# First layer of a two-layer kernel: another table of half-steps, with four stores and loads moved in SyncE's program and the products of steps 2 and 10 on GpSimd in place of 1 and 14

## The chip, the cores and the metric

The kernel runs on one core of one Trainium2 chip. The metric is the device time of one execution in microseconds, lower is better. Engines are named as in the profile: PE is TensorE's matmul (PEld its weight load), DVE is VectorE, ACT is ScalarE, POOL is GpSimd, SP (SPq in the rows) is SyncE, whose program does nothing but issue DMAs here.

## The reference, cut to what matters

Layer 0 is a windowed selective scan. The 4x128x128x128 input is cut into 8x8 windows of 64 tokens. Layer 1 is a spectral operator with a two-layer perceptron behind it; the change doesn't touch it.

```
tn = layernorm(t); xi, z = split(tn @ W_in + b_in)
xc = silu(causal_conv4(xi) + conv_b)
dr, Bm, Cm = split(xc @ W_x);  delta = softplus(dr @ dt_w + dt_b)
for each token:                                   # h: 256 channels x 16 states
    h = exp(delta * A) * h + (delta * xc) * Bm
    y = sum over the 16 states of h * Cm
y = (y + xc * D) * silu(z);  out = y @ W_out + b_out;  x1 = out + x
# layer 1: layernorm over channels, rfft2, filters, irfft2, mixing by Theta, MLP, + x1
```

## The kernel before, in words

Layer 0 works on 64 blocks, each one row of 16 windows (1024 tokens, 128 channels on the partitions). A block is 32 steps: step `n` is state `n % 16` of one half (`q = n // 16`) of the block's tokens. In a step the scan (DVE, L922) runs over 128x1024 elements with `decay` (exp(delta*A), ACT, L737) and `drive` (delta*xc*B) as inputs and writes `state`. `prod` is `state` times C, and TensorE transposes and adds each `prod` into `y_acc` (L612, `add_state`, three steps behind the scan).

Two tables say who makes what. In the even steps (`DSTEPS`) the decay lies in one PSUM buffer `decay_d`, and GpSimd makes `drive_d` (L1081) from `du` and a row of B that a DMA has broadcast into one of four `b_all`. In the odd steps ACT scales `ut` into `ub` (L750, four instructions) and PE turns it into the one buffer `drive_r` (L599, `turn_drive`). For steps in `BY_GPSIMD` the product is GpSimd's (L1092) with a row of C that a DMA has broadcast into one of four `c_all`; for the nine others it is DVE's (L933), with C broadcast by PE into `job_bank0` (L587, `broadcast_c`).

Around the scans each engine does the block's other work at half-steps: `h = 2n` is before the product at step `n`, `h = 2n + 1` behind it. `JOBS` gives PE's jobs, as (half-step, name, kind, bank): two PSUM banks are shared, a job waits until the job before it in its bank was taken, and a job in bank 0 also waits for every product of DVE of the steps before. A name's last two digits are the channel half and `q`. `mean`/`var` belong to the layernorm of the block two ahead (L629, L635), `conv`, `z`, `xp` (L641, L645, L652), `dt` (L658, the argument of softplus), `ut` and `bt` (L670, L664) prepare a block's second half or the next block, `turn` (L675 and L679) brings y back to channels, `out` (L689, L691) projects it, `fy` (L696) belongs to layer 1. `AT` gives the half-step at which ACT, DVE or GpSimd takes a job's result, and the step at which SP issues a store or an x load. All engines run their programs in order, so a wait holds everything behind it. SP's program is one queue too: `load_b` runs 8 steps ahead of its drive and `load_c` 6 steps ahead of its product, each behind a wait for its buffer, and the stores (`rows`, x1, `yo`) stand between them:

```
if n == AT["yo_out"] and S.tail:
    need(sp, s["yo_done"], m - 1)      # counted by ACT at half-step 63 of this block
    sp.dma_start(yv[...], yo[:])
...
if kind of a job: if S.bank[name] == 0:
    need(pe, s["prod_v_done"], m * len(BY_VECTOR) + nth(BY_VECTOR, n))
```

Of the kernel before, what the change touches and what calls it, by code (L numbers as in the profile page):

```python
# [62 lines left out]
RSTEPS = tuple(n for n in range(NSTEP) if n not in DSTEPS)  # L63
ALLSTEPS = tuple(range(NSTEP))
UB_AT = {}
BY_GPSIMD = (1, 3, 4, 5, 7, 8, 9, 11, 12, 13, 14, 15, 17, 18, 19, 21, 23, 24, 25, 26, 27, 29, 31)
BY_VECTOR = tuple(n for n in ALLSTEPS if n not in BY_GPSIMD)
NB, NCR, NA, ND, NS_UB, NT, NP = 4, 4, 2, 4, 2, 4, 4
B_LOAD, C_LOAD, ADD_BEHIND = 8, 6, 3
# [2 lines left out]

JOBS = [
# [8 lines left out]
]  # L82
CONV_GAP = 2
UT_BY_SCALAR = ('ut10', 'ut01', 'ut00')
Z1_BY_VECTOR = ()

AT = {

    "copy_y": (37, 8), "take_rows": (37, 2), "take_conv": (9, 19, 28, 31), "take_z": (4, 1, 18, 21),
    "softplus0": 39, "softplus1": 12, "silu": 33, "take_bt": (59, 21), "square": (43, 51), "deviation": (46, 55),  # L90
# [1 line left out]

# [2 lines left out]

# [1 line left out]

    "x_in": 17, "rows": (21, 0), "rows_landed": (22, 2), "x1_out": 15, "x_res": 14, "yo_out": 28,
}


# [5 lines left out]
def upto(steps, M, n):  # L107

    return M * len(steps) + nth(steps, n + 1)
# [7 lines left out]
def place_of(steps, M, n, ring):  # L117
    return (M * len(steps) + nth(steps, n)) % ring


def before_in(steps, M, n, ring):

    i = M * len(steps) + nth(steps, n) - ring
    return i // len(steps), steps[i % len(steps)]
# [46 lines left out]
def need(eng, sem, value):  # L171

    if isinstance(value, int) and value <= 0:
        return
    eng.wait_ge(sem, value)  # L175
# [232 lines left out]
def layer0(nc, a, wt, rows_dram, x1_dram, y_dram, blocks):  # L408
    with ExitStack() as ctx:
# [86 lines left out]
        def multiplied(eng, M, n):  # L496
            if n in BY_VECTOR:
                need(eng, s["prod_v_done"], upto(BY_VECTOR, M, n))
            else:
                need(eng, s["prod_g_done"], upto(BY_GPSIMD, M, n))  # L500

# [6 lines left out]
        def _(sp):  # L508
# [10 lines left out]
            def load_b(step):  # L519
                M, p, n = step  # L520
                q, st, slot = n // NS, n % NS, place_of(DSTEPS, M, n, NB)
                need(sp, s["drive_d_done"], upto(DSTEPS, *before_in(DSTEPS, M, n, NB)))
                sp.dma_start(b_all[slot][:], rows_dram[2 * p + q, st:st + 1, :].to_broadcast([P, HT])).then_inc(b_ready[slot], 16)

            def load_c(step):
                M, p, n = step
                q, st, slot = n // NS, n % NS, place_of(BY_GPSIMD, M, n, NCR)
                need(sp, s["prod_g_done"], upto(BY_GPSIMD, *before_in(BY_GPSIMD, M, n, NCR)))
                sp.dma_start(c_all[slot][:],
                             rows_dram[2 * p + q, NS + st:NS + st + 1, :].to_broadcast([P, HT])).then_inc(c_ready[slot], 16)  # L530
# [6 lines left out]
            def body(S, p):  # L537
# [3 lines left out]
                for n in range(NSTEP):  # L541
# [26 lines left out]
                    for k in range(NSTEP):  # L568
                        if k in DSTEPS and (k - B_LOAD) % NSTEP == n and S.step(n + B_LOAD, p):
                            load_b(S.step(n + B_LOAD, p))  # L570
                        if k in BY_GPSIMD and (k - C_LOAD) % NSTEP == n and S.step(n + C_LOAD, p):
                            load_c(S.step(n + C_LOAD, p))
# [153 lines left out]
        def _(act):  # L726
# [39 lines left out]
            def take_ut(S, hf, q):  # L766
                misc = full(act, S, f"ut{hf}{q}")
                act.activation(ut[q][:, :, hf * P:(hf + 1) * P], misc[:].rearrange("p (g d) -> p g d", g=4),
                               ACT.Copy).then_inc(take(S, f"ut{hf}{q}"), 1)
# [74 lines left out]
            def others(S, p, h):  # L844
# [9 lines left out]
                for hf in range(2):  # L854
                    if h == AT["take_ut1"][hf] and S.scan and f"ut{hf}1" in UT_BY_SCALAR:
                        take_ut(S, hf, 1)
                    if h == AT["take_ut0"][hf] and S.front and f"ut{hf}0" in UT_BY_SCALAR:
                        take_ut(S, hf, 0)
# [51 lines left out]
        def _(dve):  # L910
# [63 lines left out]
            def take_ut(S, hf, q):  # L974
                misc = full(dve, S, f"ut{hf}{q}")
                dve.tensor_copy(ut[q][:, :, hf * P:(hf + 1) * P],
                                misc[:].rearrange("p (g d) -> p g d", g=4)).then_inc(take(S, f"ut{hf}{q}"), 1)

            def take_dt(S, hf, q):
                M = S.m + 1 if q == 0 else S.m  # L980
                misc = full(dve, S, f"dt{hf}{q}")
                need(dve, s["softplus_done"], M * 8 + 4 * q + 4)
                need(dve, s["decay_d_done"], upto(DSTEPS, M - 1, NS * (q + 1) - 1))
                need(dve, s["decay_r_done"], upto(RSTEPS, M - 1, NS * (q + 1) - 1))
                need(dve, s["du_done"], (M * 2 + q - 1) * 2)
                dve.scalar_tensor_tensor(delta[:, hf, q * HT:(q + 1) * HT], misc[:], 0.0, soft[:, hf, :], ALU.max,
                                         ALU.add).then_inc(take(S, f"dt{hf}{q}"), 1)
# [31 lines left out]
            def others(S, p, h):  # L1019
# [5 lines left out]
                for hf in range(2):  # L1025
                    if h == AT["take_dt1"][hf] and S.scan:
                        take_dt(S, hf, 1)
                    if h == AT["take_dt0"][hf] and S.front:
                        take_dt(S, hf, 0)
                    if h == AT["take_ut1"][hf] and S.scan and f"ut{hf}1" not in UT_BY_SCALAR:  # L1030
                        take_ut(S, hf, 1)
                    if h == AT["take_ut0"][hf] and S.front and f"ut{hf}0" not in UT_BY_SCALAR:
                        take_ut(S, hf, 0)
# [39 lines left out]
        def _(pool):  # L1073
# [11 lines left out]
            def times_c(step):  # L1085
                M, p, n = step
                slot = place_of(BY_GPSIMD, M, n, NCR)
                M0, n0 = before_in(ALLSTEPS, M, n, NP)
# [563 lines left out]
```

## Time and profile before

| | |
|---|---|
| median of 3 runs | 9224.3 us (9222.76 to 9227.81) |
| the profiled execution | 9230.91 us, its span 9229.1 us |
| busy over the span | PE 92%, DVE 88%, ACT 83%, POOL 87% |
| layer 0 | about the first 6,650 us of the span |

The profile is one execution. A block of layer 0 is some 45 instructions on POOL, 73 on DVE, 180 on ACT. Rows name a buffer without its number, and a matmul of 512 columns of this type is counted twice (x2). PEclk is TensorE's granted clock: 1.00 is its level of 2.4 GHz and 0.50 that of 1.2 GHz.

### The profile page before, as it was taken

The page shows a single profiled execution, that of the slowest core. Times are in us where ns is not written, and L with a number is a line of the kernel's source. Part 1 is how long each engine was busy: PE and PEld are TensorE (multiplying, and loading weights), DVE is VectorE, ACT ScalarE, POOL GpSimd, SP SyncE. Part 2 cuts the span into 40 slices and gives each one's busy share as a digit, 9 for nine tenths or more (in the row PEclk, how much of TensorE's full clock was granted, in tenths as well). Part 3 has the DMA queues.
Part 4 walks back from the last instruction along what each step waited for, and adds up shares of the span by engine and source line. Part 5 has one row for each costly group of instructions (what it writes and reads, how often), then busy time and mean ns, then how long its engine had stood idle before and what let it go on. Part 6 is the DMA issues. An engine that isn't in the chain of part 4 may idle for free. (4 is left out here: it accounts for less than half of the span.)

```text
span 9229.1 us, 157478 instructions
## 1 busy us (share of the span) xinstructions
PE 8530.3 (92%) x52285; PEld 6506.9 (71%) x52285; DVE 8123.3 (88%) x8018; ACT 7644.1 (83%) x13862; POOL 8028.2 (87%) x3673
## 2 busy tenths in 40 slices
PE   6998999999999999999999999999799999999999
PEld 3666666666666666666666666666589999999788
DVE  5989988999999899989998999899789999999766
ACT  5999999999999999999999999999755555555577
POOL 4999999999999999999999999999889999999500
PEclk8999999999999999999999999999999999999999
DMA  3333334343434343434343433343310110110255
GB/s 92 118 123 127 121 121 128 120 123 120 128 120 125 120 127 118 124 120 127 120 124 119 127 120 124 120 126 122 113 36 33 37 37 33 37 37 33 89 185 182
DMA packets 675841, 982.03 MB, mean 106 GB/s; under 512 B 82762, under 2 KB 280403, under 8 KB 670931
## 3 DMA queue, kind: packets, MB, share of 16 engines
q1 hardware_dynamic: 675282, 974.98, 33.6%
q8 instruction: 302, 4.95, 0.2%
q14 instruction: 257, 2.10, 0.1%
HBM read 828.71 MB, written 146.04 MB: 106 GB/s over the span
## 5 line engine op out<-in xcount | busy, mean ns | idle before, releaser
L1092 POOL TENSOR_TENSOR prod<-state,c_all 128x1024 f32<-128x1024 f32 x1472 | 3476.0, 2374 | 95.5 <-DMA b_all<-bc_rows 54.4
L922 DVE TENSOR_TENSOR_SCAN state<-decay_r,drive_r 128x1024 f32<-128x1024 f32 x1024 | 2331.0, 2276 | 302.3 <-ACT decay_r L737 199.3
L1081 POOL TENSOR_TENSOR drive_d<-du,b_all 128x1024 f32<-128x1024 f32 x1024 | 2422.5, 2366 | 173.8 <-issue 142.7
L922 DVE TENSOR_TENSOR_SCAN state<-decay_d,drive_d 128x1024 f32<-128x1024 f32 x1024 | 2332.1, 2277 | 38.9 <-ACT decay_d L737 36.5
L612 PEld LDWEIGHTS y_acc<-ident,prod 128*128 128x128 f32 x16384 | 1918.5, 144 | 601.4 <-issue 531.1
L612 PE MATMUL y_acc<-ident,prod 128*128 128x128 f32 x16384 | 2207.0, 280 | 17.6 <-POOL prod L1092 11.5
L1369 DVE SCALAR_TENSOR_TENSOR sum_d<-bank_d,filt,sum_d 128x512 f32<-128x512 f32 x2470 | 1654.2, 742 | 119.8 <-PE bank_d L1277 119.8
L750 ACT ACTIVATE ub<-ut,bt 128x256 f32<-128x256 f32 x4096 | 1737.5, 497 | 9.3
L1416 POOL TENSOR_TENSOR sum_p<-sum_p,scaled 128x1024 f32<-128x1024 f32 x650 | 1555.2, 2393 | 79.9 <-ACT scaled L1327 32.2
L1327 ACT ACTIVATE scaled<-bank_p,filt 128x512 f32<-128x512 f32 x1560 | 944.5, 689 | 622.5 <-PE bank_p L1277 592.7
L737 ACT ACTIVATE decay_r<-delta,neg_a 128x504 f32<-128x504 f32 x2048 | 1342.0, 704 | 0.0
L737 ACT ACTIVATE decay_d<-delta,neg_a 128x504 f32<-128x504 f32 x2048 | 1310.1, 672 | 22.9 <-DVE state L922 21.1
L599 PE MATMUL drive_r<-ident,ub 128*128 128x128 f32 x8192 | 1076.0, 275 | 33.2 <-DVE state L922 27.8
L599 PEld LDWEIGHTS drive_r<-ident,ub 128*128 128x128 f32 x8192 | 928.9, 141 | 228.3 <-issue 175.2
L641 PE MATMUL job_bank<-tn,tap_w 128*128 128x512 f32 (+3 forms) x2048 | 965.9, 594 | 2.3 <-ACT zs L779 1.6
L1277 PE MATMUL bank_d<-th_high,x_high 128*128 128x256 f32 x2600 | 781.0, 300 | 6.2 <-DVE sum_d L1369 1.9
L933 DVE TENSOR_TENSOR prod<-state,job_bank 128x1024 f32<-128x1024 f32 x576 | 694.9, 1206 | 95.4 <-issue 52.5
L1277 PE MATMUL bank_d<-th_low,x_high 128*128 128x256 f32 x2600 | 735.5, 283 | 0.0
L1277 PE MATMUL bank_d<-th_high,x_low 128*128 128x256 f32 x2600 | 735.4, 283 | 0.0
L641 PEld LDWEIGHTS job_bank<-tn,tap_w 128*128 128x128 f32 x2048 | 350.2, 191 | 291.0 <-issue 272.7
L1277 PEld LDWEIGHTS bank_d<-th_high,x_high 128*128 128x128 f32 x2600 | 492.7, 190 | 37.3 <-DVE sum_d L1369 20.3
L1277 PEld LDWEIGHTS bank_d<-th_low,x_high 128*128 128x128 f32 x2600 | 492.3, 189 | 16.9 <-issue 15.3
(156 smaller groups left out, 13507.0 us busy)
## 6 DMA issues: line engine op xcount, KB each, us to landing
c_all<-bc_rows SPq DMA_DIRECT2D x1472, 256.0 KB, 3.3
b_all<-bc_rows SPq DMA_DIRECT2D x1024, 256.0 KB, 3.7
ys<-row_spectra SPq DMA_DIRECT2D x130, 256.0 KB, 2.8
column_sums<-tt SPq DMA_DIRECT2D x130, 256.0 KB, 2.2
x_in<-in_x_dram SPq DMA_DIRECT2D x64, 512.0 KB, 5.6
x_res<-in_x_dram SPq DMA_DIRECT2D x64, 512.0 KB, 4.3
x_rows<-x SPq DMA_DIRECT2D x64, 512.0 KB, 3.5
row_spectra<-z SPq DMA_DIRECT2D x64, 512.0 KB, 3.7
```

Source lines behind the costliest of these rows:

```text
L599: mm = pe.matmul(drive_r[:, hf, g * P:(g + 1) * P], ub[place_of(RSTEPS, M, n, NS_UB)][:, g, hf * P:(hf + 1) * P], wt["ident"][:], start=Tr ...
L612: mm = pe.matmul(y_acc[:, g, hf * P:(hf + 1) * P], prod[place_of(ALLSTEPS, M, n, NP)][:, hf, g * P:(g + 1) * P], wt["ident"][:], start=(n ...
L641: mm = pe.matmul(o[:, :, k:WT], wt["tap_w"][:, K - 1 - k, hf * P:(hf + 1) * P], v[:, :, 0:WT - k], start=(k == 0), stop=(k == K - 1), skip ...
L737: last = act.activation(dst[:, hf, :, 1:WT], delta[:, hf, q * HT:(q + 1) * HT].rearrange("p (w t) -> p w t", t=WT)[:, :, 1:WT], ACT.Exp, s ...
L750: last = act.activation(ub[place_of(RSTEPS, M, n, NS_UB)][:, g, :], ut[q][:, g, :], ACT.Copy, scale=bt[q][:, g, st:st + 1])
L922: dve.tensor_tensor_scan(state[place_of(ALLSTEPS, M, n, NT)][:].rearrange("p h t -> p (h t)"), decay[:].rearrange("p h w t -> p (h w t)"), ...
L1081: pool.tensor_tensor(drive_d[place_of(DSTEPS, M, n, ND)][:], du[:, :, q * HT:(q + 1) * HT], b_all[slot][:].unsqueeze(1).to_broadcast([P, 2 ...
L1092: pool.tensor_tensor(prod[place_of(ALLSTEPS, M, n, NP)][:], state[place_of(ALLSTEPS, M, n, NT)][:], c_all[slot][:].unsqueeze(1).to_broadca ...
L1277: mm = pe.matmul(o, x[p][:, part, b, :], th[:, 2 * pair:2 * pair + 2, :].rearrange("p l h -> p (l h)"), start=(b % 2 == 0 and i == 0), sto ...
L1327: act.activation(scaled[n % 2][:, i, out, :].rearrange("p (b h) -> p b h", b=B), bank_p[:, :, i, :], ACT.Copy, scale=filt[p][:, kind, 2 * ...
L1369: dve.scalar_tensor_tensor(acc, src, factor, acc, ALU.mult, ALU.add).then_inc(s["summed_d"], 1)
L1416: pool.tensor_tensor(acc, acc, scaled[n % 2][:, i], ALU.add).then_inc(s["summed_p"], 1)
```

## The change

`BY_GPSIMD` loses steps 1 and 14 and gains 2 and 10, so DVE's nine products are those of steps 0, 1, 6, 14, 16, 20, 22, 28, 30 (before: 0, 2, 6, 10, 16, 20, 22, 28, 30). `ut01` is taken by DVE instead of ACT. `JOBS` and `AT` get other half-steps nearly throughout; no work is added or removed. The core of the diff:

```diff
-BY_GPSIMD = (1, 3, 4, 5, 7, 8, 9, 11, 12, 13, 14, 15, 17, 18, 19, 21, 23, 24, 25, 26, 27, 29, 31)
+BY_GPSIMD = (2, 3, 4, 5, 7, 8, 9, 10, 11, 12, 13, 15, 17, 18, 19, 21, 23, 24, 25, 26, 27, 29, 31)
...
-    (15, "conv10", "front", 1), (16, "z01", "front", 0), (18, "ut01", "scan", 0), (20, "bt1", "scan", 0),
-    (20, "z11", "front", 1), (22, "conv01", "front", 1), (23, "ut11", "scan", 0), (25, "conv11", "front", 0),
-    (29, "out0", "back", 1), (31, "out1", "back", 0), (34, "xp0", "front", 1), (37, "dt10", "front", 0),
-    (38, "dt00", "front", 1), (40, "mean0", "ahead", 1), (45, "var0", "ahead", 0), (48, "ut00", "front", 0),
+    (15, "bt1", "scan", 1), (16, "z11", "front", 0), (16, "conv10", "front", 1), (20, "z01", "front", 0),
+    (22, "ut01", "scan", 1), (23, "ut11", "scan", 0), (24, "conv01", "front", 1), (25, "conv11", "front", 0),
+    (30, "out0", "back", 1), (31, "out1", "back", 0), (34, "xp0", "front", 1), (37, "dt00", "front", 1),
+    (38, "dt10", "front", 0), (41, "mean0", "ahead", 1), (44, "var0", "ahead", 0), (47, "ut00", "front", 0),
...
-UT_BY_SCALAR = ('ut10', 'ut01', 'ut00')
+UT_BY_SCALAR = ('ut10', 'ut00')
...
-    "x_in": 17, "rows": (21, 0), "rows_landed": (22, 2), "x1_out": 15, "x_res": 14, "yo_out": 28,
+    "x_in": 16, "rows": (18, 0), "rows_landed": (24, 2), "x1_out": 21, "x_res": 19, "yo_out": 31,
```

Three places of the new order matter below. On PE, around the `mean0` job (L629) in the second half of a block; L658 are the two `dt` jobs, L635 is `var0`, L670 is `ut00`, L612 the adds, L599 the turned drives, L587 the broadcasts of C. Before:

```order
L658 MATMUL job_bank<-rows,dt_w 128x512 x2
L612 MATMUL y_acc<-ident,prod 128x128 x8
L599 MATMUL drive_r<-ident,ub 128x128 x8
L629 MATMUL job_bank<-x_in,centre_w 128x512
L612 MATMUL y_acc<-ident,prod 128x128 x8
L587 MATMUL job_bank<-c_rows,pick 128x512
L612 MATMUL y_acc<-ident,prod 128x128 x8
L599 MATMUL drive_r<-ident,ub 128x128 x8
L612 MATMUL y_acc<-ident,prod 128x128 x8
L635 MATMUL job_bank<-sq,mean_w 128x512
L587 MATMUL job_bank<-c_rows,pick 128x512
```

And now:

```order
L658 MATMUL job_bank<-rows,dt_w 128x512 x2
L612 MATMUL y_acc<-ident,prod 128x128 x8
L599 MATMUL drive_r<-ident,ub 128x128 x8
L612 MATMUL y_acc<-ident,prod 128x128 x8
L629 MATMUL job_bank<-x_in,centre_w 128x512
L587 MATMUL job_bank<-c_rows,pick 128x512
L612 MATMUL y_acc<-ident,prod 128x128 x8
L599 MATMUL drive_r<-ident,ub 128x128 x8
L635 MATMUL job_bank<-sq,mean_w 128x512
L612 MATMUL y_acc<-ident,prod 128x128 x8
L587 MATMUL job_bank<-c_rows,pick 128x512
L612 MATMUL y_acc<-ident,prod 128x128 x8
L670 MATMUL job_bank<-ident,du 128x128 x4
```

One add moved ahead of `mean0`, and `var0` moved ahead of an add. `ut00` (L670) now follows the broadcast for step 22 with one add between.

On SP, at the end of a block, around the store of `yo` (L554); L523 loads a row of B, L529 one of C, L534 and L535 store a half block's rows. Before:

```order
L523 DMA b_all<-bc_rows 128x512
L529 DMA c_all<-bc_rows 128x512
L554 DMA row_spectra<-z 128x8x128
L523 DMA b_all<-bc_rows 128x512
L529 DMA c_all<-bc_rows 128x512 x2
L523 DMA b_all<-bc_rows 128x512
L529 DMA c_all<-bc_rows 128x512
L534 DMA bc_rows<-rows 16x512
L535 DMA bc_rows<-rows 16x512
```

And now:

```order
L523 DMA b_all<-bc_rows 128x512
L529 DMA c_all<-bc_rows 128x512 x2
L523 DMA b_all<-bc_rows 128x512
L554 DMA row_spectra<-z 128x8x128
L529 DMA c_all<-bc_rows 128x512
L534 DMA bc_rows<-rows 16x512
L535 DMA bc_rows<-rows 16x512
```

The store stands behind the loads of B for steps 4 and 6 and of C for 2, 3 and 4 now, where it stood ahead of B for 4 and 6 and of C for 3, 4 and 5.

On DVE, in the middle of a block, steps 10 to 16 (scans L922, `decay_d` in even steps; L933 a product; L976 a take of `ut`). Before:

```order
L922 SCALAR_TENSOR_TENSOR state<-decay_d,drive_d 128x1024
L922 SCALAR_TENSOR_TENSOR state<-decay_r,drive_r 128x1024
L933 TENSOR_TENSOR prod<-state,job_bank 128x1024
L922 SCALAR_TENSOR_TENSOR state<-decay_d,drive_d 128x1024
L976 COPY ut<-job_bank 128x4x128
L922 SCALAR_TENSOR_TENSOR state<-decay_r,drive_r 128x1024
L922 SCALAR_TENSOR_TENSOR state<-decay_d,drive_d 128x1024
L922 SCALAR_TENSOR_TENSOR state<-decay_r,drive_r 128x1024
L1004 TENSOR_TENSOR x<-job_bank,out_b_rows 128x512
```

And now:

```order
L922 SCALAR_TENSOR_TENSOR state<-decay_d,drive_d 128x1024
L922 SCALAR_TENSOR_TENSOR state<-decay_r,drive_r 128x1024
L976 COPY ut<-job_bank 128x4x128 x2
L922 SCALAR_TENSOR_TENSOR state<-decay_d,drive_d 128x1024
L922 SCALAR_TENSOR_TENSOR state<-decay_r,drive_r 128x1024
L922 SCALAR_TENSOR_TENSOR state<-decay_d,drive_d 128x1024
L922 SCALAR_TENSOR_TENSOR state<-decay_r,drive_r 128x1024
L933 TENSOR_TENSOR prod<-state,job_bank 128x1024
```

Both takes of `ut` now stand between scans 11 and 12, and a product follows scan 15 instead of scan 11.

## Rows read from the trace of the kernel before

**Rows 1.** Layer 0: stretch, its length, busy PE, PEld, DVE, ACT, POOL, PEclk, DMA.

```profile
1000.00:3000.00 2000.00, 1830.46 (x10742) 1295.98 (x10743) 1819.42 (x1406) 1874.90 (x3494) 1885.64 (x881) 0.98 0.39 123
```

**Rows 2.** The same view for three whole blocks.

```profile
3893.79:3995.07 101.28, 92.74 (x552) 66.12 (x549) 92.87 (x73) 95.73 (x179) 96.70 (x46) 0.98 0.40 124
4097.86:4201.20 103.34, 94.61 (x552) 66.48 (x550) 92.84 (x73) 95.81 (x179) 96.33 (x46) 0.97 0.40 121
2776.00:2876.20 100.20, 91.48 (x551) 64.89 (x550) 92.56 (x73) 95.72 (x180) 96.29 (x45) 1.00 0.41 125
```

**Rows 3.** Who waited for whom, 2000 to 4000 us: total us, times, longest.

```profile
DVE state L922 <- ACT decay_r L737: 63.3, 20, 3.2
POOL drive_d L1081 <- issue: 49.1, 16, 3.9
PE job_bank L675 <- DVE delta L986: 40.7, 19, 2.1
```

**Rows 4.** The same view for SP's own queue.

```profile
SPq L554 <- ACTq L842: 163.1, 20, 8.5
```

**Rows 5.** SP in order of time, turn of a block: start us, us, instruction.

```profile
3894.52 0.39 SPq L554 DMA_DIRECT2D row_spectra<-z  x1
3894.95 0.58 SPq L523 DMA_DIRECT2D b_all<-bc_rows  x1
```

**Rows 6.** POOL in order of time; [idle before <-releaser].

```profile
3900.62 2.36 POOL L1081 TENSOR_TENSOR drive_d<-du,b_all 128x1024 f32<-128x1024 f32 x1 [2.76 <-issue]
```

**Rows 7.** Busy time in three stretches of the block that starts at 3893.87.

```profile
3893.87:3916.72 22.85, 20.62 (x111) 13.28 (x109) 22.09 (x15) 22.36 (x43) 20.09 (x10) 1.00 0.51 138
3916.72:3954.90 38.18, 38.07 (x237) 28.27 (x237) 31.70 (x27) 36.79 (x67) 38.18 (x20) 1.00 0.34 114
3967.13:3995.14 28.01, 25.26 (x169) 19.08 (x167) 27.78 (x19) 24.44 (x50) 27.32 (x13) 0.99 0.27 87
```

**Rows 8.** PE in order of time, the wait for `dt01` in this block.

```profile
3916.72 1.12 PE L675 MATMUL job_bank<-xc,diag_d 128*128 128x512 f32 x2 [2.15 <-DVE delta L986]
3922.15 1.02 PE L645 MATMUL job_bank<-tn,z_w 128*128 128x512 f32 x2
```

**Rows 9.** The same place one block earlier.

```profile
3813.53 1.70 PE L675 MATMUL job_bank<-xc,diag_d 128*128 128x512 f32 x2 [2.14 <-DVE delta L986]
3820.53 1.02 PE L645 MATMUL job_bank<-tn,z_w 128*128 128x512 f32 x2
```

**Rows 10.** Busy time and granted clock in two short stretches.

```profile
3814.00:3817.40 3.40, 3.40 (x10) 1.83 (x9) 1.26 (x3) 3.40 (x8) 3.40 (x2) 0.51 0.47 159
3964.30:3967.50 3.20, 3.20 (x14) 2.43 (x13) 2.67 (x3) 3.20 (x8) 3.20 (x2) 0.50 0.01 3
```

**Rows 11.** PE in order of time, around `mean0`.

```profile
3958.99 1.09 PE L599 MATMUL drive_r<-ident,ub 128*128 128x128 f32 x8 [0.32 <-DVE state L922]
3962.73 1.12 PE L629 MATMUL job_bank<-x_in,centre_w 128*128 128x512 f32 x2 [2.65 <-DVE delta L986]
3963.69 1.48 PE L612 MATMUL y_acc<-ident,prod 128*128 128x128 f32 x8
3965.10 0.79 PE L587 MATMUL job_bank<-c_rows,pick 48*128 48x512 f32 x1
```

**Rows 12.** DVE in order of time, same place.

```profile
3961.98 1.29 DVE L986 SCALAR_TENSOR_TENSOR delta<-job_bank,soft 128x512 f32<-128x512 f32 x2 [0.34 <-issue]
3963.19 2.28 DVE L922 TENSOR_TENSOR_SCAN state<-decay_r,drive_r 128x1024 f32<-128x1024 f32 x1
3965.99 1.22 DVE L933 TENSOR_TENSOR prod<-state,job_bank 128x1024 f32<-128x1024 f32 x1 [0.53 <-DVE state L922]
```

**Rows 13.** ACT in order of time, same place.

```profile
3960.84 1.06 ACT L791 ACTIVATE soft<-soft 128x1024 f32<-128x1024 f32 x1
3970.38 0.60 ACT L806 ACTIVATE sq<-job_bank 128x512 f32<-128x512 f32 x1 [2.04 <-PE job_bank L635]
```

**Rows 14.** A group of instructions, 2000 to 4000 us: busy us, mean ns, idle before.

```profile
L976 DVE COPY ut<-job_bank 128x512 f32<-128x512 f32 x19 | 12.7, 666 | 0.0
```

More of the change, by code:

```diff
@@ L74 @@
     (0, "z10", "front", 0), (0, "xp1", "scan", 1), (3, "z00", "front", 1), (4, "conv00", "front", 1),
[7 rows of a table removed]
[7 rows of a table added]
 ]
 CONV_GAP = 2
-UT_BY_SCALAR = ('ut10', 'ut01', 'ut00')
+UT_BY_SCALAR = ('ut10', 'ut00')
 Z1_BY_VECTOR = ()
 AT = {
-    "copy_y": (37, 8), "take_rows": (37, 2), "take_conv": (9, 19, 28, 31), "take_z": (4, 1, 18, 21),
-    "softplus0": 39, "softplus1": 12, "silu": 33, "take_bt": (59, 21), "square": (43, 51), "deviation": (46, 55),
[4 rows of a table removed]
-    "x_in": 17, "rows": (21, 0), "rows_landed": (22, 2), "x1_out": 15, "x_res": 14, "yo_out": 28,
+    "copy_y": (37, 7), "take_rows": (35, 2), "take_conv": (10, 20, 30, 32), "take_z": (3, 1, 21, 18),
+    "softplus0": 39, "softplus1": 11, "silu": 34, "take_bt": (57, 15), "square": (44, 53), "deviation": (45, 56),
[4 rows of a table added]
+    "x_in": 16, "rows": (18, 0), "rows_landed": (24, 2), "x1_out": 21, "x_res": 19, "yo_out": 31,
 }
```

14 rows, old and new, of tables (AT, JOBS) are left out of this document.

## The prediction

> **What bounds the kernel now.** I looked first at where the time per block goes. POOL runs 45 instructions a block, so its 881 in 2,000 us are 19.6 blocks, 102.15 us each [rows 1]. POOL is busy 94% of that, ACT 94%, PE and DVE 91%: no engine is full, and the shares don't say which waits set the end. Blocks also differ: 100.20 us where the granted clock is 1.00 all along, 101.28 at 0.98, 103.34 at 0.97 [rows 2]. So I took one block apart and asked of each engine where it has no gap. After its first 22.85 us, in which DVE is busy for 22.09, PE takes over and works 38.07 of 38.18 us without a gap [rows 7]. Then ACT makes the softplus of the next block's first half (its Ln ends at 3961.90 [rows 13]) and DVE's take of it starts at 3961.98 [rows 12]; from the scan at 3967.13 to the next block's first scan DVE is busy for 27.78 of 28.01 us [rows 7]. That is the ring that sets a block: DVE, PE, ACT's softplus, DVE. POOL isn't in it. Its one large gap, 2.76 us ahead of a drive [rows 6] and 2.5 us a block on average (49.1 us in 19.6 blocks [rows 3]), is made by SP: the store of `yo` waits 8.2 us a block for ACT's last instruction of the block (163.1 us, 20 times [rows 4]), and the row of B for step 4 is issued right behind it, at 3894.95 [rows 5], 5.7 us before the drive starts. But the scans don't wait for that drive: no row of scans behind POOL stands among the long waits.
>
> PE itself waits twice in each block for a take by DVE of a `dt` job in its bank: 2.1 us at L675 [rows 3, 8] and 2.65 us at L629 [rows 11]. Behind each the clock can fall. In one block the granted clock was 0.51 after the wait at L675 [rows 10], and from L675 to L645 it took 7.00 us [rows 9]; in the next block, undisturbed, 5.43 [rows 8]: a fall costs 1.57. After the wait at L629 it was 0.50 [rows 10], and the add behind `mean0` took 1.48 us and the broadcast 0.79 [rows 11]. As the 101.28 block has this second fall and no first one, the second costs 101.28 - 100.20 = 1.08 us, and a first one 1.57 to 2.06 (103.34 - 101.28) more [rows 2]. The average of 102.15 is then a second fall in nearly every block and a first one in (102.15 - 101.28) / 2.0, some 45% of them.
>
> **The change part by part.** The products: DVE keeps nine and POOL 23, at 1.2 and 2.3 us each, so no engine's sum changes but by `ut01`, 0.67 us more on DVE and about as much less on ACT [rows 14].
>
> First stretch (DVE, 22.85 us). Product 2 becomes product 1 and `turn10` goes ahead of `turn_drive(5)`. Scan 5 now waits about 1 us for that turn, but the gate that stood behind scan 5 is done in that gap. I come out at 22.9, +0.05.
>
> Middle (PE, 38.18 us). PE's jobs are reordered, none is added; broadcast 10 goes and broadcast 14 comes in the same stretch. Of 38.18 us 0.11 were a wait [rows 7] for the take ahead of broadcast 10: it goes. Is there a new wait? `bt1` stands first now, and ACT must take it before the `conv10` behind it in bank 1; ACT waits there for some 1.3 us instead of at `z01`, and PE not at all by my count. `ut11`, `conv11` and broadcast 14 find their banks taken 0.4 to 1.3 us ahead. DVE has both takes of `ut` ahead of scan 12, 0.67 us each, and product 14 behind scan 15. Scan 15 waits 3.2 us for PE's turned drive (63.3 us over 20 [rows 3]), so both takes are hidden by that wait, and product 14 by PE's 5 us of `out0` and `out1`. Cost 0; uncovered, the takes would be 0.67 us. Value -0.05 for the middle.
>
> Softplus. `take_rows` goes ahead of an ub, so ACT has no other work ahead of the softplus; it still starts with the copy of y, which waits for PE's add 15. The sum gives the end of Ln 0.2 us earlier, with what the middle gave.
>
> Behind the take (the largest term). Product 20 waited for its broadcast, which stood behind `mean0` and an add at the low clock: 0.53 us of wait in the row, and 0.6 from start to start [rows 12]. The add now stands ahead of `mean0`, in PE's wait of 2.65 us, which shrinks by its 0.9 to about 1.75. The broadcast comes right behind `mean0`: by DVE's rows the product can start 3.4 us after the take (1.21 and 2.20 from start to start [rows 12]), and `mean0` and the broadcast need some 2.5 of these, at the low clock. So even a fall there costs nothing, and with the shorter wait it may not come. That is worth 1.08 us in blocks that had it, nearly all: 1.05 on average. `var0` ahead of an add takes ACT's wait of 2.04 us [rows 13] away; since DVE is full there it gives slack, not time. What is late next is `ut00`: it must wait for product 22, now just ahead, about 2.1 us. Behind it stand turned drive 25, `turn01` and `mean1`. Scan 25 wants that drive 2.8 us after product 22 (a scan and a take of `tn`), and `ut00` and the drive need 1.5 at full clock and 3.1 at half: 0 to 0.3, I take 0.1.
>
> SP. The store behind the loads takes POOL's gap of 2.5 us away. No stretch of the ring holds POOL, so I take 0; bounds are 0 and the whole 2.5 (a rival, below). The `rows` store three steps earlier stands behind `take_rows`, done 10 us before; the x loads move by two and five steps and land well ahead.
>
> The first fall. The wait at L675 stays 2.1 us, and nothing says in which blocks the fall behind it comes; with another block length it falls on others. Its bounds are none (-0.9 us a block against now) and all (+1.0, the other 55% at 1.8). I take 60 to 65%, above today's 45%: +0.3.
>
> **The sum**: +0.05 - 0.05 - 0.2 - 1.05 + 0.1 + 0.3 = -0.85 us a block. Over 64 blocks -54 us. Against the profiled execution's own 9230.91 that is 9177; its 6.6 us above the median of 9224.3 are kept, so the median should be 9170. What measurement can tell from no change is about 0.2%, 18 us.
>
> **The rivals.** (1) POOL is what binds, and the moved store is the gain. It is the busiest engine, and its gap is real; against it, its releases come early, and among the long waits none is for it. It would give 2.5 us a block, -160 us: 9064. The Trainium skill (Perfetto Trace Analysis, Identifying the Most-Contended Engine) has it so: the engine with the highest occupancy is the one to optimize first. Here that engine is POOL by a hair, and the rows of the ring speak against it. Chance 5%. (2) No change: the fall behind L675 comes in nearly every block once the other is gone, +1.0 instead of +0.3 a block, and what is left is -0.15 a block, 9214. For it: the wait isn't touched and the block length is what chooses. Chance 14%. (3) Slower, by DVE's middle: with two takes and later the product the scans 12 to 14 run late. If the 3.2 us ahead of scan 15 were used up, because ACT's new wait for `bt1` pushes decays 10 to 14 by more than 3.2 - 1.3 = 1.9 us, each further us would be 64 us: from 0.85 us on the gain is gone, and with 1.4 us it is 35 us slower, 9259. For it: decay 10 and 14 are single-buffered and close behind their scans. Against it: PE reaches `bt1` right behind the first adds. Chance 11%. (4) The fall behind L675 becomes rare: -0.65 us a block instead of +0.3, together -1.8, 9109. Chance 8%.
>
> **Numbers.** The forecast keeps 62%, from 9130 to 9206. With (2) and (4) it holds some eight in ten, so the range is 9105 to 9216. Faster by over 0.2% is the forecast, (1), (4) and a bit more: 0.76; within 0.2% 0.13; slower 0.11.
>
> **What the profile would show.** Right: the wait of ACT for L635 (2.0 us) and DVE's wait ahead of product 20 gone; PE's wait at L629 1.7 to 1.8 us; a new wait of about 2 us at L670; POOL's gap at the drive gone with POOL's other gaps longer by the same; blocks with clock 1.00 at 100.0 us, and others 1.6 to 2 us longer. Wrong: full-clock blocks far below 100 (then POOL was in the ring), or at 101 and more with the wait ahead of scan 15 gone (3), or 102 on average at a clock of 0.97 (2).

## The result: 9153.4 us, 0.8% faster, and the profile after

| | before | after |
|---|---|---|
| median of 4 runs each | 9225.7 us (9222.8 to 9227.8) | 9153.4 us (9148.6 to 9160.7) |
| ratio | | 0.9921, 95% interval 0.9909 to 0.9934 |
| the profiled execution | 9230.9, span 9229.1 | 9160.7, span 9158.9 |

The forecast was 9170 in a range of 9105 to 9216. The change takes off 72 us, where the sum said 54.

The same stretch as in [rows 1], and two blocks one behind the other (columns as there):

```profile
1000.00:3000.00 2000.00, 1842.83 (x10854) 1315.95 (x10855) 1842.82 (x1433) 1886.10 (x3511) 1909.17 (x891) 0.98 0.40 124
2649.42:2749.30 99.88, 91.51 (x551) 65.07 (x549) 93.06 (x74) 95.28 (x178) 96.46 (x46) 1.00 0.40 126
2749.30:2850.81 101.51, 93.97 (x551) 67.84 (x549) 93.24 (x75) 95.26 (x178) 96.53 (x46) 0.97 0.39 124
```

POOL's 891 instructions at 45 a block are 19.8 blocks, 101.0 us each (102.15 before). A block at full clock has gone from 100.20 to 99.88; one with both falls, 103.34 in [rows 2], now lasts 101.51.

PE around `mean0` in the second of these blocks, one with a low clock there, against [rows 11]:

```profile
2816.74 1.04 PE L612 MATMUL y_acc<-ident,prod 128*128 128x128 f32 x8
2819.38 1.13 PE L629 MATMUL job_bank<-x_in,centre_w 128*128 128x512 f32 x2 [1.59 <-DVE delta L986]
2820.43 0.50 PE L587 MATMUL job_bank<-c_rows,pick 48*128 48x512 f32 x1
2820.86 1.80 PE L612 MATMUL y_acc<-ident,prod 128*128 128x128 f32 x8
2822.45 1.91 PE L599 MATMUL drive_r<-ident,ub 128*128 128x128 f32 x8
```

DVE in the same place, against [rows 12]:

```profile
2818.63 1.29 DVE L986 SCALAR_TENSOR_TENSOR delta<-job_bank,soft 128x512 f32<-128x512 f32 x2 [0.16 <-issue]
2819.84 2.28 DVE L922 TENSOR_TENSOR_SCAN state<-decay_r,drive_r 128x1024 f32<-128x1024 f32 x1
2822.03 1.20 DVE L933 TENSOR_TENSOR prod<-state,job_bank 128x1024 f32<-128x1024 f32 x1
```

The wait at L629 is 1.59 us instead of 2.65. The clock falls behind it all the same: the add takes 1.80 us and the turned drive 1.91, about 1.04 at full clock. But the broadcast is out by 2820.93, and product 20 has no wait: 2.19 us from scan to product where it was 2.80. That is the step on which the prediction put most.

The long waits, 2000 to 4000 us, against [rows 3], and SP's own against [rows 4]:

```profile
PE job_bank L675 <- DVE delta L986: 43.2, 20, 2.2
PE job_bank L670 <- issue: 33.0, 20, 2.1
PE job_bank L629 <- DVE delta L986: 31.9, 20, 1.6
DVE state L922 <- PE drive_r L599: 41.8, 50, 3.0
DVE state L922 <- ACT decay_r L737: 27.2, 9, 3.0
```

```profile
SPq L554 <- ACTq L842: 6.8, 20, 0.6
```

The wait at L675 is as long as before, and that at L670 is new, 1.65 us on average. The 3 us ahead of scan 15 is still there; it is put down now to PE, now to ACT. SP waits 0.3 us a block for `yo` instead of 8.2, and POOL has no row of waits for a drive any more.

### The profile page after: what moved, and what is told of

It reads as the page before. It is cut to its first block and busy times, and to the rows that moved or that the text cites. A ratio compares the mean times of both kernels' runs of the same rounds, so it can differ in the third digit from the quotient of the medians.

```text
span 9158.9 us, 157541 instructions
## 1 busy us (share of the span) xinstructions
PE 8504.2 (93%) x52285; PEld 6526.3 (71%) x52285; DVE 8151.9 (89%) x8082; ACT 7618.8 (83%) x13798; POOL 8038.0 (88%) x3673
## 5 line engine op out<-in xcount | busy, mean ns | idle before, releaser
L922 DVE TENSOR_TENSOR_SCAN state<-decay_r,drive_r 128x1024 f32<-128x1024 f32 x1024 | 2328.9, 2274 | 244.7 <-PE drive_r L599 149.9
L922 DVE TENSOR_TENSOR_SCAN state<-decay_d,drive_d 128x1024 f32<-128x1024 f32 x1024 | 2329.8, 2275 | 79.6 <-ACT decay_d L737 79.6
L612 PEld LDWEIGHTS y_acc<-ident,prod 128*128 128x128 f32 x16384 | 1894.1, 143 | 609.5 <-issue 514.1
L612 PE MATMUL y_acc<-ident,prod 128*128 128x128 f32 x16384 | 2199.3, 278 | 20.4 <-POOL prod L1092 6.4
L599 PE MATMUL drive_r<-ident,ub 128*128 128x128 f32 x8192 | 1100.4, 279 | 59.5 <-DVE state L922 40.4
L599 PEld LDWEIGHTS drive_r<-ident,ub 128*128 128x128 f32 x8192 | 946.0, 143 | 199.0 <-issue 136.7
L641 PE MATMUL job_bank<-tn,tap_w 128*128 128x512 f32 (+3 forms) x2048 | 941.3, 587 | 0.8 <-ACT zs L779 0.8
L933 DVE TENSOR_TENSOR prod<-state,job_bank 128x1024 f32<-128x1024 f32 x576 | 691.5, 1200 | 7.2 <-issue 1.8
```

Source lines behind the costliest of these rows:

```text
L599: mm = pe.matmul(drive_r[:, hf, g * P:(g + 1) * P], ub[place_of(RSTEPS, M, n, NS_UB)][:, g, hf * P:(hf + 1) * P], wt["ident"][:], start=Tr ...
L612: mm = pe.matmul(y_acc[:, g, hf * P:(hf + 1) * P], prod[place_of(ALLSTEPS, M, n, NP)][:, hf, g * P:(g + 1) * P], wt["ident"][:], start=(n ...
L641: mm = pe.matmul(o[:, :, k:WT], wt["tap_w"][:, K - 1 - k, hf * P:(hf + 1) * P], v[:, :, 0:WT - k], start=(k == 0), stop=(k == K - 1), skip ...
L922: dve.tensor_tensor_scan(state[place_of(ALLSTEPS, M, n, NT)][:].rearrange("p h t -> p (h t)"), decay[:].rearrange("p h w t -> p (h w t)"), ...
```

## Blocks, and where the clock falls

The averages hide what differs from block to block, so I sorted the same 56 blocks of each profile (the sixth to the sixty-first) by the trace's record of the granted clock. A first fall comes 20 to 30 us into the block, behind L675; a second at 66 to 75 us, at `mean0`; a late one at 76 to 84 us, behind the wait at L670. The table holds the experiments too; ratios are to the kernel before, run on the same chip. "Mean block" is taken over all 63 distances from one block's first scan to the next block's; the falls are counted in the 56. "Clean" is the length of a block without a fall.

| kernel | median us | ratio, 95% interval | mean block | clean (how many) | first | second | late |
|---|---|---|---|---|---|---|---|
| before | 9225.7 | | 102.20 | 100.2 (3) | 27 | 53 | 0 |
| after | 9153.4 | 0.9921 (0.9909 to 0.9934) | 101.05 | 99.9 (21) | 33 | 22 | 7 |
| e1 before + SP's positions | 9223.1 | 0.9999 (0.9990 to 1.0008) | 102.06 | 100.2 (5) | 25 | 51 | 0 |
| e2 before + second half | 9235.3 | 1.0007 (0.9998 to 1.0016) | 102.24 | 100.2 (1) | 54 | 0 | 55 |
| e3 before + first half | 9463.5 | 1.0263 (1.0249 to 1.0277) | 105.88 | none | 4 | 56 | 0 |
| e4 after + add 4 early | 9077.6 | 0.9839 (0.9826 to 0.9853) | 99.76 | 99.5 (19) | 0 | 12 | 25 |
| e5 before + mean0 at 41 | 9188.3 | 0.9948 (0.9935 to 0.9962) | 101.45 | 100.2 (15) | 41 | 23 | 0 |
| e6 before + first half and SP | 9200.6 | 0.9963 (0.9949 to 0.9976) | 101.86 | 99.9 (8) | 27 | 48 | 0 |
| e7 after, mean0 at 40 | 9190.4 | 0.9951 (0.9938 to 0.9965) | 101.69 | none | 31 | 44 | 13 |
| e8 after, yo at 28 | 9203.8 | 0.9979 (0.9970 to 0.9988) | 101.83 | 100.9 (1) | 36 | 10 | 35 |
| e9 after + adds 4, 5 early | 9037.8 | 0.9785 (0.9772 to 0.9798) | 99.10 | 99.0 (45) | 0 | 7 | 4 |
| e10 before + adds 4, 5 early | 9236.3 | 1.0015 (1.0006 to 1.0024) | 102.31 | 100.8 (4) | 1 | 52 | 0 |
| e11 e9, bt1 later | 9033.4 | 0.9794 (0.9781 to 0.9807) | 99.11 | 99.0 (37) | 0 | 11 | 8 |
| e12 e10 + SP's positions | 9166.9 | 0.9932 (0.9918 to 0.9946) | 101.20 | none | 0 | 56 | 0 |

The median of before lay between 9225 and 9236 from one set of runs to the next, so differences below are read from ratios. In e3 and in e8 one more fall, at 39 us of a block, is in no column.

In the kernel before, a block with the second fall alone lasts 101.41 on average and one with both 103.21: 1.21 for the second, 1.80 for the first. In the kernel after, a first fall costs 1.58 (101.45 against 99.87), a second 0.05 (101.50 against 101.45), and a late one 1.0 to 1.4.

## The experiments

**The change in three parts.** The tables fall apart into SyncE's positions, the first half of the block (`BY_GPSIMD`, `UT_BY_SCALAR`, jobs below half-step 34 and what takes them), and the second half.

e1, SyncE's positions alone:

```diff
-    "x_in": 17, "rows": (21, 0), "rows_landed": (22, 2), "x1_out": 15, "x_res": 14, "yo_out": 28,
+    "x_in": 16, "rows": (18, 0), "rows_landed": (24, 2), "x1_out": 21, "x_res": 19, "yo_out": 31,
```

> The kernel before with SyncE's six positions of the change alone (the store of yo at step 31 instead of 28, and the rows, x1 and x loads as changed). My theory: POOL's gap at the drive behind that store goes and nothing else does, so the time stays within 18 us of before's 9225.7. Rival, POOL binds: 2.5 us a block less, 9066. A third way: the scans' times move a little and the clock falls in other blocks, up to 30 us either way.

Measured: no difference. SP's wait for `yo` fell as in the changed kernel, and POOL's gap at the drive is gone:

```profile
SPq L554 <- ACTq L842: 14.1, 20, 1.0
```

```profile
POOL xc L1110 <- ACT xc L779: 53.8, 20, 2.8
```

What POOL won it waits away for ACT, at L1110 (53.8 us over 20 blocks, 2.7 each; 9.9 us in all before), and the block is as long as before. POOL isn't what binds there: the rule of the Trainium skill (Perfetto Trace Analysis, Identifying the Most-Contended Engine) that was rival 1 would have looked in the wrong place, though POOL is the busiest of the four engines in every profile of layer 0 here.

e2, the second half alone (`mean0` 41, `dt00` ahead of `dt10`, `var0` 44, `ut00` 47, `turn01` 48, `mean1` 49, `var1` 54, `bt0` and `ut10` 57, and what takes them):

```diff
-    (38, "dt00", "front", 1), (40, "mean0", "ahead", 1), (45, "var0", "ahead", 0), (48, "ut00", "front", 0),
+    (38, "dt10", "front", 0), (41, "mean0", "ahead", 1), (44, "var0", "ahead", 0), (47, "ut00", "front", 0),
...
```

> The kernel before with the change's positions of the block's second half alone (the add ahead of mean0, dt00 ahead of dt10, var0, ut00, turn01, mean1, var1, bt0, ut10 and what takes them). My theory: this part carries the gain, 1.1 to 1.2 us a block, so about 9225.7 - 72 = 9154, and at the least 9175 if the first clock fall comes in more blocks. Rival, the gain comes from the first half or from the store: within 18 us of before.

Measured: no gain. My theory in that form fell; the rival has the number but not the reason, since e5 below gains 0.52% by one number of this half. Three blocks of it (columns as in [rows 1]):

```profile
2257.37:2359.77 102.40, 94.25 (x552) 66.62 (x550) 92.74 (x73) 95.94 (x179) 96.28 (x46) 0.97 0.37 123
2359.77:2462.16 102.39, 94.22 (x551) 66.58 (x550) 92.74 (x73) 95.92 (x179) 96.28 (x46) 0.97 0.40 123
2567.32:2667.54 100.22, 91.51 (x551) 65.00 (x549) 92.56 (x74) 95.68 (x179) 95.37 (x46) 1.00 0.39 125
```

The second fall is gone in all 56 blocks, as it should be. But the first comes in 54 and a late one in 55, at the same 22.9 and 80.9 us of every block, and each block is 102.4 us long: once this length is reached, it repeats. That is rival 2 of the prediction (the first fall in nearly every block), which the whole change escaped.

e3, the first half alone, with SyncE's positions as before:

```diff
-BY_GPSIMD = (1, 3, 4, 5, 7, 8, 9, 11, 12, 13, 14, 15, 17, 18, 19, 21, 23, 24, 25, 26, 27, 29, 31)
+BY_GPSIMD = (2, 3, 4, 5, 7, 8, 9, 10, 11, 12, 13, 15, 17, 18, 19, 21, 23, 24, 25, 26, 27, 29, 31)
...
```

> The kernel before with the change's first half alone (products 1 and 14 on DVE instead of 2 and 10, bt1, z11, z01, the two takes of ut, turn10, conv, x1). My theory: nothing, since PE's stretch in the middle keeps its jobs: within 18 us of before's 9225.7. Rival, the removed wait ahead of broadcast 10 and the other order carry the gain: about 9155.

Measured: 2.6% slower, which neither the theory nor the rival had. The waits, 2000 to 4000 us, one of SP's among them:

```profile
PE job_bank L629 <- DMA x_in<-in_x_dram: 96.0, 19, 5.4
```

```profile
SPq L562 <- DVE stats L1011: 144.4, 19, 7.9
```

DVE's statistics stand two half-steps later in the new first half. The x1 store at step 15 waits for them, 7.6 us a block instead of 4.4 (87.7 us over 20 before), the x load stands behind it, and PE waits 5 us a block for the x load. The first half can't do without SyncE's positions. Which of them it needs was not run one by one; the waits point to the x1 store and the x load behind it.

e6, the first half with SyncE's positions (the changed kernel with the second half as before):

```diff
-    (38, "dt10", "front", 0), (41, "mean0", "ahead", 1), (44, "var0", "ahead", 0), (47, "ut00", "front", 0),
+    (38, "dt00", "front", 1), (40, "mean0", "ahead", 1), (45, "var0", "ahead", 0), (48, "ut00", "front", 0),
...
```

> The changed kernel with the second half of the block as before, that is the kernel before with the first half and SyncE's positions of the change together. My theory: the 236 us by which the first half alone was slower came from SyncE's old positions, where the x1 store waited 7.9 us for DVE's statistics and held the x load; with the new positions they go, and what is left is the gain of a full-clock block, 0.3 us, with the fall behind mean0 still there: 9225 - 20 = 9205, between 9180 and 9240 by the number of first falls. Rival, the first half is slow with the old second half whatever SyncE does: over 9400.

Measured: 0.37% faster, with clean blocks of 99.9. The 236 us are gone with SyncE's positions, and the 0.3 us of a clean block come from the first half: with SyncE's positions alone (e1) a clean block stays at 100.2.

**The one number.** e5, the kernel before with the add ahead of `mean0`:

```diff
-    (38, "dt00", "front", 1), (40, "mean0", "ahead", 1), (45, "var0", "ahead", 0), (48, "ut00", "front", 0),
+    (38, "dt00", "front", 1), (41, "mean0", "ahead", 1), (45, "var0", "ahead", 0), (48, "ut00", "front", 0),
```

> The kernel before with a single number changed: mean0 at half-step 41 instead of 40, so that the add of step 17 stands ahead of it on PE. My theory, after the run with the whole second half: the wait at L629 shrinks from 2.65 to 1.7 us, the clock fall behind it and the wait ahead of product 20 go, and a block without the first fall lasts 100.2 us instead of 101.4. The time then hangs on the first fall alone: 102.0 us a block if it comes in every block as it did there, which would be 9220, and 101.0 a block, 9150, if it comes in half of them. Rival, the single add does nothing and the other moves of the second half took the second fall away: 9225, with the fall at 70 us into the block still there.

Measured: 0.52% faster, inside the theory's 9150 to 9220. PE's wait and the broadcast behind it:

```profile
2418.81 1.12 PE L629 MATMUL job_bank<-x_in,centre_w 128*128 128x512 f32 x2 [1.79 <-DVE delta L986]
2419.87 0.49 PE L587 MATMUL job_bank<-c_rows,pick 48*128 48x512 f32 x1
```

A second fall costs 0.27 here (102.05 with both, 101.78 with the first alone) instead of 1.21, and comes in 23 blocks instead of 53; the theory had it gone. First falls went from 27 to 41, which gave part of it back.

e7, the reverse: the changed kernel with `mean0` at 40.

```diff
-    (38, "dt10", "front", 0), (41, "mean0", "ahead", 1), (44, "var0", "ahead", 0), (47, "ut00", "front", 0),
+    (38, "dt10", "front", 0), (40, "mean0", "ahead", 1), (44, "var0", "ahead", 0), (47, "ut00", "front", 0),
```

> The changed kernel with mean0 back at half-step 40, ahead of the add of step 17. My theory: the wait at L629 is 2.5 us again and the fall behind it comes in nearly every block and costs about 1.1 us: 9153 + 65 = 9218, less what a different number of first falls gives back. Rival, with product 20's broadcast still early and DVE's order as it is, the fall costs nothing: 9153 to 9165.

Measured: 0.30% slower than the changed kernel, some 27 us where the theory had 65 and the rival at most 12. Second falls went from 22 to 44 and cost 0.8 to 1.0 again (100.7 with the second alone against the changed kernel's 99.9). The gain of e5 and that of e6, 0.52 and 0.37%, add up to the 0.79% of the change within the intervals.

**The store of yo.** e8, the changed kernel with one number back:

```diff
-    "x_in": 16, "rows": (18, 0), "rows_landed": (24, 2), "x1_out": 21, "x_res": 19, "yo_out": 31,
+    "x_in": 16, "rows": (18, 0), "rows_landed": (24, 2), "x1_out": 21, "x_res": 19, "yo_out": 28,
```

> The changed kernel with the store of yo alone back at step 28, ahead of the loads of B and C. My theory: SyncE waits some 8 us a block there again and POOL's drive behind the store is 2 to 3 us late, but no scan waits for it: within 15 us of the changed kernel's 9153. Rival: with product 2 now on GpSimd, whose load of C also stands behind the store, the late row reaches the scans of steps 4 to 6 and costs 1 us a block, 9217.

Measured: 0.6% slower than the changed kernel, some 50 us. My theory fell. The size is near the rival's 64, by another way than it named. One block (PE and DVE at the `ut` jobs, POOL at the drives):

```profile
2053.83 4.71 POOL L1081 TENSOR_TENSOR drive_d<-du,b_all 128x1024 f32<-128x1024 f32 x2 [4.26 <-issue]
...
2084.41 0.63 PE L670 MATMUL job_bank<-ident,du 128*128 128x128 f32 x4 [1.80 <-POOL du L1099]
...
2085.08 0.69 DVE L976 COPY ut<-job_bank 128x512 f32<-128x512 f32 x1 [2.54 <-PE job_bank L670]
```

POOL is 4.26 us late at the drive behind the store. Its `du` of the second channel half (the changed table makes it three half-steps later than before, at 21) comes late, PE waits 1.80 us for it ahead of `ut11`, DVE 2.54 us for `ut11`, and in the changed order both takes stand ahead of scan 12. The average of DVE's wait is 1.2 (23.5 us in 19 waits, against 11.1 in 20). It hangs on the first fall. In the 21 of the 56 blocks without one DVE waits 2.0 us for `ut`, and they last 101.8 on average instead of the changed kernel's 100.0; in the 35 with one, PE comes to `ut11` late anyway, DVE waits 0.65, and they last 101.9 instead of 101.7. So most of the loss is that a block without a first fall is no longer a short one. Late falls came in 35 blocks instead of 7; their share is not told apart.

**The wait at L675.** e4 does to it what the change did to L629. The add of step 4 goes ahead of `turn11`; in the changed kernel it stands behind the broadcast of step 6:

```diff
-                    if S.step(n - ADD_BEHIND, p):
-                        add_state(S.step(n - ADD_BEHIND, p))
+                    for k in [k for k in {6: (3, 4), 7: ()}.get(n, (n - ADD_BEHIND,)) if S.step(k, p)]:
+                        add_state(S.step(k, p))
```

> The changed kernel with one more add moved in the same way: the add of step 4, which stands behind the broadcast for step 6, goes ahead of turn11, into PE's wait of 2.15 us at L675 (the product of step 4 is ready before that wait starts). My theory: the wait shrinks to about 1.3 us, the clock fall behind it goes as that behind mean0 went with a wait of 1.6, and PE's full stretch in the middle has 0.9 us less work: 1.6 us in six of ten blocks and 0.9 in all, 1.8 us a block, 9153 - 115 = 9040. Rival, only the fall goes and something else in the middle takes the 0.9: 9153 - 60 = 9093. Rival, the fall does not depend on this wait: 9153 - 58 = 9095 without any change in the number of falls. Rival, no change: 9153.

e9, the changed kernel with the adds of steps 4 and 5 both early:

```diff
-                    if S.step(n - ADD_BEHIND, p):
+                    for k in [k for k in {6: (3, 4, 5), 7: (), 8: ()}.get(n, (n - ADD_BEHIND,)) if S.step(k, p)]:
```

> The changed kernel with the adds of steps 4 and 5 both ahead of turn11 (the run with the add of step 4 alone gave 9077.6). PE's wait at L675 was 1.3 us there and would be about 0.4. My theory: that run's gain was the first fall and little of PE's 0.9 us (its blocks last 99.5 against 99.9), because the scans of the middle wait 3.0 us for something else by now; a second add then gives nothing in the middle, and the time stays within 15 us of 9078. Rival, PE's stretch in the middle still sets the end: another 0.9 us a block, 9020. Rival, product 5 isn't ready, PE waits for POOL, and it gets slower, 9100.

Measured: 9077.6 and 9037.8 us, 1.6 and 2.15% faster than before. e9's whole stretch and one block of it, and PE at `turn11`:

```profile
1000.00:3000.00 2000.00, 1857.22 (x11093) 1315.34 (x11094) 1878.77 (x1474) 1919.86 (x3577) 1949.76 (x910) 1.00 0.41 127
2496.52:2595.50 98.98, 91.89 (x551) 65.09 (x549) 92.93 (x75) 95.07 (x178) 96.47 (x46) 1.00 0.40 127
```

```profile
2516.17 2.87 PE L612 MATMUL y_acc<-ident,prod 128*128 128x128 f32 x24
2519.37 1.12 PE L675 MATMUL job_bank<-xc,diag_d 128*128 128x512 f32 x2 [0.33 <-DVE delta L986]
...
2521.72 0.52 PE L664 MATMUL job_bank<-ident,rows 88*128 88x88 f32 x4 [0.36 <-DVE gated L992]
...
2532.39 0.63 PE L670 MATMUL job_bank<-ident,du 128*128 128x128 f32 x4 [0.21 <-POOL du L1099]
```

With a wait of 1.3 us (e4) or 0.33 (e9) no first fall is left in any block. The clean block goes from 99.9 to 99.5 to 99.0: PE's stretch in the middle was in the ring, as the prediction had it, and each add taken out of it is worth 0.4 to 0.5 us. It isn't the whole 0.87 of an add. Part of the rest can be seen: with the first add moved PE waits 0.36 us for the gate to take the bank ahead of `bt1`, and with the second 0.21 more ahead of `ut11` for POOL's `du`. e4 took off 0.8% of the changed kernel's time, some 75 us: less than the 115 of its theory (9040), more than the 60 of its rivals. For e9 the measured time lies between my theory, which was within 15 us of 9078, and the rival of 9020: I had taken the middle for no longer binding, and it was.

e11, e9 with that 0.36 filled:

```diff
-    (15, "bt1", "scan", 1), (16, "z11", "front", 0), (16, "conv10", "front", 1), (20, "z01", "front", 0),
+    (16, "bt1", "scan", 1), (16, "z11", "front", 0), (17, "conv10", "front", 1), (20, "z01", "front", 0),
```

> The changed kernel with both adds ahead of turn11, and bt1 behind the turned drive of step 9 instead of ahead of it, so that PE does not wait 0.36 us there for the gate to take bank 1. My theory: PE's stretch in the middle sets the end, so this gives 0.36 us a block, 9037.8 - 23 = 9015. Rival, ACT takes bt later and the takes of decay follow: within 8 us of 9038. Rival, a new wait in the middle: slower than 9046.

Measured: as e9, with the same clean block of 99.0; the first rival's time came. PE's waits in the middle, 2000 to 4000 us:

```profile
PE job_bank L645 <- DVE prod L933: 4.9, 20, 0.3
PE job_bank L670 <- POOL du L1099: 4.3, 20, 0.2
```

Of the 0.36 us PE loses 0.25 again, ahead of `z11` (L645), waiting for DVE's product. `ut11` starts at 35.9 us of a clean block as in e9, behind the same wait for POOL's `du`. So the wait that was filled is not the one that ended last there.

e10, the kernel before with the edit of e9, and e12, that of e10 with the table line of e1:

> The kernel before with the adds of steps 4 and 5 ahead of turn11 and nothing of the change. My theory: the first fall goes (about 0.9 us a block on average there) and PE's full stretch is up to 0.9 us shorter in its result; with the second fall at 70 us left in nearly every block, 102.2 - 0.9 - 0.9 = 100.4 us a block, 9225 - 115 = 9110. Rival, the change is needed for it (product 5 or the gates are late in the old order): above 9170. Rival, the second fall goes as well: 9040.

> The kernel before with SyncE's positions of the change and the adds of steps 4 and 5 ahead of turn11: two edits that gave nothing each by itself (9223.1 and 9236.3). My theory: the two adds gave nothing because the late store made POOL 2.7 us late, so that PE waited 1.2 us for product 5 in place of the wait that the adds were to fill. With the store moved that wait goes, the first fall stays away, and PE's stretch in the middle is 0.9 us shorter in its result, with the fall behind mean0 left: 102.2 - 0.9 - 0.9 = 100.4 us a block, 9225 - 115 = 9110; up to 9140 if the middle gives only 0.4. Rival, POOL's lateness has nothing to do with it (the old order of products, the gates): 9215 to 9240 again.

e10 gave 0.15% more time, not 1.2% less: its rival, that the change is needed for it, has the number. One of its blocks, POOL at the drive behind the store, and PE at the second add:

```profile
3399.09 2.36 POOL L1081 TENSOR_TENSOR drive_d<-du,b_all 128x1024 f32<-128x1024 f32 x1 [2.72 <-issue]
...
3410.70 4.71 POOL L1092 TENSOR_TENSOR prod<-state,c_all 128x1024 f32<-128x1024 f32 x2
...
3415.46 1.09 PE L612 MATMUL y_acc<-ident,prod 128*128 128x128 f32 x8 [1.23 <-POOL prod L1092]
3416.40 1.02 PE L675 MATMUL job_bank<-xc,diag_d 128*128 128x512 f32 x2
```

The first fall is gone (1 block of 56), but PE waits 1.23 us for product 5, since POOL lost 2.72 at the drive, and `turn11` comes 1.2 us late. In e12 the store is out of the way and PE waits only for the take:

```profile
2567.16 1.13 PE L675 MATMUL job_bank<-xc,diag_d 128*128 128x512 f32 x2 [0.39 <-DVE delta L986]
```

It is 0.68% faster than before. Two edits that gave nothing apart, 0.01% less and 0.15% more, give 63 us together. It is less than the 115 of my theory: a second fall is in all 56 blocks, and they last 101.27 on average, hardly less than the 101.41 of before's blocks with that fall alone. Two of them, one behind the other:

```profile
924.60:1025.31 100.71, 93.05 (x551) 66.18 (x549) 92.48 (x73) 95.63 (x179) 96.35 (x46) 0.98 0.40 125
1025.31:1127.33 102.02, 94.35 (x551) 66.88 (x549) 92.68 (x73) 95.64 (x179) 96.74 (x46) 0.97 0.40 123
```

The middle did get shorter: `mean0` starts 68.3 us into the block instead of 68.9. Where the fall begins 1 us behind that start, as in the first of these blocks, a block lasts 100.8 on average (19 of 56), against 101.3 to 101.4 in the kernel before. But in 37 of the 56 the fall begins 0.3 to 1.0 us ahead of `mean0`, in PE's wait of 2.65 us, and these blocks last 101.5 on average, the second of the two 102.0. So the gain of the middle is there, and much of it is lost to falls that come earlier.

## Why the prediction was right

By its own terms, from the table (56 blocks, in which the mean went from 102.21 to 100.98):

| term | predicted | measured |
|---|---|---|
| first stretch | +0.05 | 0.01: from first scan to the takes of `dt` 22.14 us (22.13) |
| middle and softplus | -0.25 | -0.32: from first scan to the next takes 67.79 (68.11) |
| behind the take, second fall | -1.05 | -1.13: 53 x 1.21 of 56 before, 22 x 0.05 after |
| `ut00`'s new wait | +0.1 | 0 in clean blocks, +0.16 by 7 late falls |
| first fall | +0.3 | +0.06: 27 x 1.80 before, 33 x 1.58 after |
| sum | -0.85 | -1.2; over all 63 blocks -1.15 |

The second column's first two terms come from two clean blocks. DVE's first scan, the takes of the second half and those of the next block, before:

```profile
2770.72 2.28 DVE L922 TENSOR_TENSOR_SCAN state<-decay_d,drive_d 128x1024 f32<-128x1024 f32 x1
...
2792.85 1.26 DVE L986 SCALAR_TENSOR_TENSOR delta<-job_bank,soft 128x512 f32<-128x512 f32 x2
...
2838.83 1.29 DVE L986 SCALAR_TENSOR_TENSOR delta<-job_bank,soft 128x512 f32<-128x512 f32 x2 [0.34 <-issue]
```

And after:

```profile
2649.42 2.28 DVE L922 TENSOR_TENSOR_SCAN state<-decay_d,drive_d 128x1024 f32<-128x1024 f32 x1
...
2671.56 1.26 DVE L986 SCALAR_TENSOR_TENSOR delta<-job_bank,soft 128x512 f32<-128x512 f32 x2
...
2717.21 1.29 DVE L986 SCALAR_TENSOR_TENSOR delta<-job_bank,soft 128x512 f32<-128x512 f32 x2 [0.19 <-issue]
```

**The large term held, mechanism and size.** The wait at L629 was 1.6 (forecast 1.7 to 1.8), product 20 waits no longer, and e5 and e7 show the one number behind it in both tables. That the fall "may not come" with the shorter wait was half right: it comes in 22 blocks, and costs 0.05 because the broadcast is already out.

**The mis-sized terms.** The first fall came in 33 of 56 blocks, 59%, where I had 60 to 65; but it also costs 0.2 less than it did. The prediction used one price, 1.8, for both kernels. The lower price and the late falls, which the prediction did not have, nearly cancel. That the share of first falls came out close is luck: the prediction had no way to tell it ("nothing says in which blocks"), and 54 of 56 as in e2 would have cost another 0.6 us a block (21 x 1.58 in 56), half of the gain. Softplus and the middle gave 0.07 more, `ut00` in clean blocks 0.1 less.

**A step that held only in its setting.** "I take 0" for the moved store is right for the kernel before (e1) and wrong as a statement on the change: with the store left at 28, the changed kernel is 50 us slower (e8), and with all of SyncE's positions left as before its first half is 236 us slower than before (e3). The prediction went over SP too fast: it gives the load of `x_in` two steps where the table has one, and does not name the x1 store, which moves by six. It is that store, at its old place, behind which the x load of e3 stands. POOL isn't in the ring of the kernel before, but with the store at 28 it is too late for `ut11` in the new order. The sum came out because the change has both, the new order and the new positions.

**Rivals.** POOL as the bound fell with e1. No change by more first falls did not come, but e2 shows that it was real: the second half alone runs into it. Slower by DVE's middle fell: scan 15 still waits 3.0 us (3.2 before), so ACT's wait for `bt1` was covered. First falls becoming rare did not come with this change, and did with one add more.

## What to carry to other kernels

Where an engine waits for a release that can't come earlier, put work into the wait that already stands ready behind it: one add into each of two waits gave 0.5% and 0.8% here, the second one on top of the change. It pays twice, since the stretch behind gets shorter, and the clock falls less often behind the shorter wait.

A queue's store that holds a busy engine can cost nothing and still forbid the next improvement. Test an edit that gave nothing again with its partner, and look at the block lengths one by one: an average of 102.2 was three kinds of block.

## What the runs showed of the hardware

**The clock falls behind short waits, not in every block.** Behind the wait of 2.1 to 2.2 us at L675 it fell in 25 to 54 of 56 blocks, in eight kernels (e3, with a like wait, had 4); with 1.3 us or less there (e4, e9, e11, e12) in none. In e10, where PE waits for a product there instead (31.4 us in 34 waits, 2000 to 4000 us), it fell in one. At `mean0` it fell in 44 to 56 blocks with a wait of 2.2 to 2.7 us (before, e1, e6, e7, e10, e12), and in 0 to 23 with 1.5 to 1.8. The Trainium skill (TensorE: Matmul & The Clock Gate, A second HAM failure mode: psum-queue depth-cycling) says that an engine that pauses often and briefly between groups of matmuls can swing between the two levels; these profiles agree. The wait is not all that decides, as e3 shows, and a fall can begin inside the wait (e12). A first or second fall cost between 0.05 us, where the result was already out, and 1.8.

**A block's length chooses its falls.** In e2 each block was 102.4 us long and had its falls at the same places; in the changed kernel blocks of 101.5 and 99.9 us take turns over long stretches. So an edit that gives 1 us in one place can bring a fall in another, and the time must be read with the falls counted. Before a run I could not say in which blocks they would come, and after it I can only count them.
